# Two scratch tables in HBM stored with the heads as rows, and read back in 512-byte pieces

## The chip, the core and the metric

The kernel runs on one core of a Trainium2 chip. The metric is the device time of one execution in microseconds, in a median over runs. The core has a matrix engine (PE, with its weight loads listed as PEld), a vector engine (DVE), an activation engine (ACT), a general engine (POOL) and a queue engine (SP) that here only issues transfers. Sixteen DMA engines of the core carry out the transfers that SP and ACT issue.

## What is computed

The reference is one layer of a state-space mixer with a feed-forward part, on 2 sequences of 512 tokens with 512 channels. What bears on this case is the decay between tokens of a chunk:

```python
dt = clip(softplus(dt + dt_bias), 0, 100);  A_dt = dt * -exp(A_log)
A_cum = cumsum(A_dt, axis=-1)              # within a chunk of 128 tokens, per head
L = exp(_segsum(A_dt))                     # exp(A_cum[l] - A_cum[s]) for s <= l
Y_diag = einsum('bzlhn,bzshn,bhzls,bzshp->bzlhp', Cc, Bc, L, xch)
Y_off  = einsum('bzlhn,bzhpn,bhzl->bzlhp', Cc, prev, exp(A_cum))
```

There are 128 heads of 64 channels, 8 chunks of 128 tokens (4 of each sequence), and 8 groups that share B and C. Before this stands the input projection (512 to 18,560 columns), a causal convolution of 4 taps and a SiLU; behind it a gate, a group norm, the output projection (8192 to 512), a layer norm, a linear layer with low-rank additions and a second layer norm.

## The kernel before

A short first part, some 70 us long, projects the time steps (DT) and the first group's tiles, and computes the running sums A_cum for all heads at once: a tile of 128 heads x 1024 tokens (`sc[2]`) and its exponential (`sc[3]`). ACT writes both to scratch tables in HBM: `acum_d` (line 843) and `eacum_d` (line 857, in two transfers, even heads and odd heads). ACT also writes the small table `elast_d` (line 859).

Then come 8 groups of 16 steps. A step is a chunk c of a unit e (8 heads). Everything in the steps is laid out in the program; nothing is planned at run time, and each engine works through its own list, held by semaphores. In every step

- SP issues the loads in a fixed order (lines 448 to 470): `decay` for a later step, `eac` for the step after next where the chunk isn't a sequence's first, then the next weight tiles (`raw`, line 379), and now and then output weights (`wo_raw`, `c_new`, line 388) and a unit's small tables (`uch`, `tok`, `elast`).
- The load of `decay` (line 356) copies the A_cum of 8 heads of a chunk, 4 KB, to each of the 128 partitions. There are three slots: one for odd chunks, two for even ones. The load for an odd chunk is issued two steps ahead, for an even one four steps ahead, both once PE has read the slot's old content (`yd_ready`).
- The load of `eac` (line 365) copies exp(A_cum) of 4 heads, 2 KB, to each of 64 partitions, twice (even heads to the lower half, odd heads to the upper half).
- ACT subtracts (line 791, function `gaps`) and exponentiates (line 797) the decay, DVE multiplies it by C B^T (line 1125), and PE multiplies it with the inputs (line 654, `p_yd`). DVE scales the part from the state by `eac` (line 1151), and POOL adds it (line 1004).
- PE projects the weight tiles of the next unit: ACT rounds a loaded tile (`w_hi`, line 709), POOL takes the rest (`w_lo`, line 952), and PE does three matmuls of each (lines 495 to 497). A `raw` slot is loaded anew once both halves were taken from it.

`acum_d` lies by chunk first: (8 chunks, 128 heads, 128 tokens). `eacum_d` lies by chunk, then by even or odd head, then by head. So the 8 heads of a unit are contiguous within a chunk, and so are its 4 even ones.

Of the kernel before, what the change touches and what calls it, by code (L numbers as in the profile page):

```python
# [16 lines left out]
F32 = mybir.dt.float32  # L17
# [5 lines left out]
P = 128  # L23
BATCH, SEQ, HID = 2, 512, 512
TOK = BATCH * SEQ
KC = HID // P
HEADS, HD, NST, GROUPS, TAPS = 128, 64, 128, 8, 4
INTER = HEADS * HD
CHUNKS = TOK // P
CPB = CHUNKS // BATCH  # L30
UNITS = 2 * GROUPS
UH = HEADS // UNITS
UT = UH * HD // P
# [47 lines left out]
def wait(eng, sem, value):  # L81

    if not (isinstance(value, int) and value <= 0):
        eng.wait_ge(sem, value)
# [8 lines left out]
def mixer_ffn_kernel(nc, x_t, x_tok, w_t, unit_chan, group_chan, dt_bias, a_log, wo_t,  # L93
                     ffn_w, lora_a, lora_b, lora_w, ffn_bias, eye, upper, out):
    ctx = ExitStack()
    with ctx:
        def sb(name, shape, dt=F32):
            return ctx.enter_context(nc.sbuf_tensor(name, shape, dt))

        def sem(name):  # L100
            return ctx.enter_context(nc.semaphore(name))

        def pair(name):
            return [sem(f"{name}{i}") for i in range(2)]


        acum_d = nc.dram_tensor("acum_d", (CHUNKS, HEADS, P), F32, kind="Internal").ap()
        eacum_d = nc.dram_tensor("eacum_d", (CHUNKS, 2, HEADS // 2, P), F32, kind="Internal").ap()
        elast_d = nc.dram_tensor("elast_d", (HEADS, CHUNKS), F32, kind="Internal").ap()
        tok_d = nc.dram_tensor("tok_d", (P, UNITS, 3 * CHUNKS * UH), F32, kind="Internal").ap()  # L110

# [13 lines left out]
        decay = sb("decay", [P, 3, UH, P])  # L125
        eac = sb("eac", [P, 2, UT, P])
# [41 lines left out]
        raw_loaded, wo_loaded, decay_loaded, eac_loaded = pair("raw_loaded"), [sem(f"wo_loaded{i}") for i in range(UT)], [sem(f"decay_loaded{i}") for i in range(3)], pair("eac_loaded")  # L168
# [19 lines left out]
        acum_stored, eacum_stored, toks_stored = sem("acum_stored"), sem("eacum_stored"), sem("toks_stored")  # L188
# [11 lines left out]
        sc = [hs[:, 1, k, :] for k in range(UT)] + [half[:, 2 * k:2 * k + 2, :].rearrange("p a b -> p (a b)") for k in range(4)]  # L200
# [18 lines left out]
        def step(g, e, c):  # L219
            return g * 16 + (8 * e + c)  # L220

        def carried(g, e, c):

            return g * 12 + (6 * e + 3 * (c // CPB) + c % CPB)
# [18 lines left out]
        def dslot(c):  # L243

            return 0 if c % 2 else 1 + c // 2 % 2
# [105 lines left out]
        def load_decay(q, g, e, c):  # L351


            wait(q, yd_ready, step(g, e, c) - (1 if c % 2 else 3))
            src = acum_d[c, (2 * g + e) * UH:(2 * g + e + 1) * UH, :]
            q.dma_start(decay[:, dslot(c)].rearrange("p a b -> p (a b)"),
                        bass.AP(tensor=src.tensor, offset=src.offset, ap=[[0, P], [1, UH * P]])).then_inc(decay_loaded[dslot(c)], 16)

        def load_eac(q, g, e, c):

            slot = (carried(0, e, c) - 1) % 2
            wait(q, dh_ready, step(g, e, c) - 1)
            for h2 in range(2):
                src = eacum_d[c, h2, (2 * g + e) * UT:(2 * g + e + 1) * UT, :]
                q.dma_start(eac[h2 * HD:(h2 + 1) * HD, slot].rearrange("p a b -> p (a b)"),
                             bass.AP(tensor=src.tensor, offset=src.offset,
                                     ap=[[0, HD], [1, UT * P]])).then_inc(eac_loaded[slot], 16)


        @block.sync  # L370
        def _(sp):
# [37 lines left out]

            sp.wait_ge(acum_stored, 16)  # L410
            load_decay(sp, 0, 0, 0)
            load_w(None, PROLOGUE[9])
            load_decay(sp, 0, 0, 2)
            load_w(None, PROLOGUE[10])
            load_decay(sp, 0, 0, 1)
            sp.wait_ge(eacum_stored, 48)
            for slot in range(2):
                sp.wait_ge(unit_loaded[slot], 16)
                load_elast(sp, slot, slot)
            load_eac(sp, 0, 0, 1)  # L420
            load_w(0, LOOP_TILES[0])
            sp.wait_ge(tok_laid, 4)
# [24 lines left out]
            def body(g, last):  # L447
                for e in range(2):
                    for c in range(8):
                        od, ed, cd = ahead(e, c, 2 if c % 2 else 4)  # L450
                        if not (last and od):
                            load_decay(sp, g + od, ed, cd)
                        o2, e2, c2 = ahead(e, c, 2)
                        if c2 % CPB and not (last and o2):
                            load_eac(sp, g + o2, e2, c2)
                        for t in tiles_of(e, c, last):
                            off, n = divmod(t.n + 4, GRP_TILES)
                            if not (last and off):
                                load_tile(g + off, LOOP_TILES[n], last)
                        if c == 7 and not last:  # L460
                            load_channels(sp, 2 * g + (e + 2), e)
                            load_unit(sp, 2 * g + (e + 2), e)
                        if e == 0 and c == 4 and not last:
                            load_group(sp, g + 1)
                        if last and (e, c) == (1, 1):

                            sp.wait_ge(gated, step(GROUPS - 1, 1, 0))
                            for dst, src in ((ffn_w_sb, ffn_w), (lora_a_sb, lora_a), (lora_b_sb, lora_b),
                                             (bias_sb, bass.AP(tensor=ffn_bias.tensor, offset=0, ap=[[0, P], [1, HID]])),
                                             (lw[:], lora_w)):  # L470
                                sp.dma_start(dst, src).then_inc(ffn_loaded, 16)
# [231 lines left out]
        def _(act):  # L703
# [7 lines left out]
            def drain_proj(g, t, items=(0, 1)):  # L711

                for i, b in enumerate(t.batches):
                    if i not in items:
                        continue
                    act.wait_ge(proj_ready, item_n(g, t, i) + 1)
                    src = proj[bank(t, i)][:]
                    u, us = unit_of(g, t), uslot_of(t)
                    cols = slice(b * SEQ, (b + 1) * SEQ)
                    if t.kind in ("G0", "G1"):  # L720

                        wait(act, gated, 8 * u if t.kind == "G1" else 8 * u - 4)
                        nc.scalar.activation(gate[:, b, t.j, :], src, ACT.Silu).then_inc(proj_free[bank(t, i)], 1)
                        continue
                    if t.kind == "H":
                        wait(act, gated, 8 * u - 8)
                        dst, w, bias = hs[:, us, t.j, cols], conv_w(us, t.j, 3), conv_w(us, t.j, 4)
                        act.wait_ge(unit_loaded[us], chan_count(g, t))
                    else:
                        k = "BC".index(t.kind)  # L730
                        if t.kind == "C":
                            wait(act, c_ready, 0 if g is None else 2 * g + 2)
                            wait(act, wo_lo_ready, 0 if g is None else (2 * g + 2) * UT)
                        dst, w, bias = (bT, c_new)[k][:, cols], gch[:, k, 3:4], gch[:, k, 4:5]
                        act.wait_ge(group_loaded, 16 if g is None else 16 * g + 32)
                    nc.scalar.activation(dst, src, ACT.Identity, scale=w, bias=bias).then_inc(tap3_done, 1)  # L736
# [103 lines left out]
            drain_proj(None, PROLOGUE[4])  # L840
            silus(None, [PROLOGUE[3]])
            act.wait_ge(scanned, 2)
            act.dma_start(acum_d.rearrange("c h l -> h c l"), sc[2].rearrange("h (c l) -> h c l", c=CHUNKS)).then_inc(acum_stored, 16)
            drain_proj(None, PROLOGUE[5], (0,))
            v = sc[4].rearrange("p (c l) -> p c l", c=CHUNKS)
            a = sc[2].rearrange("p (c l) -> p c l", c=CHUNKS)
# [6 lines left out]
            nc.scalar.activation(sc[3], sc[2], ACT.Exp).then_inc(act_pre, 1)  # L853
            lay_tokens(1, 0)
            act.wait_ge(act_pre, 7)
            for h2 in range(2):
                act.dma_start(eacum_d[:, h2].rearrange("c a l -> a c l"),
                              sc[3][h2:HEADS:2].rearrange("a (c l) -> a c l", c=CHUNKS)).then_inc(eacum_stored, 16)
            act.dma_start(elast_d, elc[:]).then_inc(eacum_stored, 16)
            drain_proj(None, PROLOGUE[6], (0,))  # L860
            lay_tokens(2, 2)
# [540 lines left out]
```

## Time and profile before

| | |
|---|---|
| median of 3 runs | 1650.03 us (1648.02 to 1651.37) |
| the profiled execution | 1651.37 us, its span 1648.4 us |
| PE busy | 1614.3 us, 98% of the span |
| PEld, DVE, ACT, POOL busy | 78%, 82%, 74%, 62% |
| granted clock of PE, mean | 0.996 |
| DMA | 178.65 MB in 87144 packets, 108 GB/s over the span |

Each engine's row in the profile gives the time in which it had an instruction under way. Matmuls overlap one another, so that a busy PE is one with work in it, and not one at its peak. A DMA packet is here one piece of a transfer that is contiguous on both sides. The time "to landing" of a transfer runs from its issue to the last of its bytes, with the work that lay ahead of it in the DMA engines.

### The profile page before, as it was taken

How to read it: one execution, taken by the hardware profiler on the slowest of the kernel's cores; microseconds unless marked ns; L12 is line 12 of the kernel's file. 1: busy time of each engine (PE TensorE's matmuls, PEld its weight loads, DVE VectorE, ACT ScalarE, POOL GpSimd, SP SyncE). 2: the span in 40 equal slices, each digit the busy share in tenths (PEclk: the TensorE clock that was granted, in tenths of full speed). 3: DMA queues.
4: the chain of work that ended last, by engine and by line, in shares of the span. 5: the costliest groups of instructions: out<-in, count | busy, mean ns of one | idle time of the engine just before them, and what ended most of it. 6: DMA issues, size and time to landing. Idle time of an engine off the chain costs nothing. (4 is left out here: it accounts for less than half of the span.)

```text
span 1648.4 us, 26983 instructions
## 1 busy us (share of the span) xinstructions
PE 1614.3 (98%) x9072; PEld 1292.7 (78%) x9072; DVE 1348.8 (82%) x1855; ACT 1221.5 (74%) x2373; POOL 1021.2 (62%) x829
## 2 busy tenths in 40 slices
PE   7999999999999999999999999999999999999898
PEld 6777888778888788878887788887887878877655
DVE  5677798869987799877988689986998879887876
ACT  5868778776777877776787777788677778777742
POOL 4456667566675757656665656756566666666654
PEclk9999999999999999999999999999999999999999
DMA  3633324333242333423243333433323332333301
GB/s 125 238 110 103 113 84 157 88 103 103 84 158 84 113 96 107 132 91 113 92 123 118 99 100 94 145 97 113 99 100 120 103 119 94 108 110 102 128 27 45
DMA packets 87144, 178.65 MB, mean 108 GB/s; under 512 B 16480, under 2 KB 20576, under 8 KB 86624
## 3 DMA queue, kind: packets, MB, share of 16 engines
q1 hardware_dynamic: 83760, 175.72, 33.7%
q8 instruction: 73, 1.20, 0.3%
q10 hardware_dynamic: 3248, 1.22, 0.3%
q14 instruction: 63, 0.52, 0.1%
HBM read 172.17 MB, written 4.72 MB: 107 GB/s over the span
## 5 line engine op out<-in xcount | busy, mean ns | idle before, releaser
L952 POOL TENSOR_TENSOR w_lo<-raw,w_hi 128x512 fp32r<-128x512 f32 x209 | 297.9, 1426 | 295.5 <-ACT w_hi L709 294.5
L495 PE MATMUL proj<-x_hi,w_hi 128*128 128x512 f32 x1160 | 462.8, 399 | 8.5 <-DVE x_lo L1216 6.9
L496 PE MATMUL proj<-x_lo,w_hi 128*128 128x512 f32 x1160 | 452.9, 390 | 0.0
L497 PE MATMUL proj<-x_hi,w_lo 128*128 128x512 f32 x1160 | 452.8, 390 | 0.0
L1103 DVE SCALAR_TENSOR_TENSOR hs<-proj,uch,hs 128x511 f32<-128x511 f32 (+2 forms) x384 | 285.4, 744 | 56.9 <-ACT hs L736 51.6
L791 ACT ACTIVATE decay<-decay,tok 128x128 f32<-128x128 f32 x1024 | 312.5, 392 | 0.0
L1004 POOL TENSOR_TENSOR dh<-dh,eac 128x512 f32<-128x512 f32 x96 | 127.8, 1331 | 228.5 <-DVE eac L1151 228.4
L495 PEld LDWEIGHTS proj<-x_hi,w_hi 128*128 128x128 f32 x1160 | 218.9, 189 | 50.8 <-issue 6.9
L1125 DVE TENSOR_TENSOR decay<-decay,cb 128x1024 f32<-128x1024 f32 x128 | 190.9, 1491 | 80.2 <-ACT decay L797 77.7
L497 PEld LDWEIGHTS proj<-x_hi,w_lo 128*128 128x128 f32 x1160 | 218.3, 188 | 46.0
L496 PEld LDWEIGHTS proj<-x_lo,w_hi 128*128 128x128 f32 x1160 | 219.0, 189 | 41.6
L542 PE MATMUL p_out<-wo_hi,g_hi 128*128 128x512 f32 x512 | 211.7, 413 | 4.8 <-issue 4.8
L544 PE MATMUL p_out<-wo_hi,g_lo 128*128 128x512 f32 x512 | 201.8, 394 | 0.0
L543 PE MATMUL p_out<-wo_lo,g_hi 128*128 128x512 f32 x512 | 200.7, 392 | 0.0
L736 ACT ACTIVATE hs<-proj,uch 128x512 f32<-128x512 f32 x128 | 99.3, 776 | 133.0 <-PE proj L497 131.7
L1047 POOL TENSOR_TENSOR y<-y,gate 128x512 f32<-128x512 f32 x128 | 169.3, 1323 | 17.7 <-DVE y L1266 17.6
L709 ACT ACTIVATE w_hi<-raw 128x512 fp32r<-128x512 f32 x196 | 122.3, 624 | 68.8 <-PE proj L497 68.5
L969 POOL TENSOR_TENSOR xd<-xdt,tok 128x512 f32<-128x512 f32 x96 | 147.9, 1540 | 1.6 <-DVE xdt L1114 1.6
L975 POOL TENSOR_TENSOR dh<-hs,uch 128x512 f32<-128x512 f32 x128 | 148.4, 1159 | 0.7 <-ACT hs L746 0.7
L654 PE MATMUL p_yd<-decay,xdt 128*64 128x128 f32 x2048 | 140.1, 279 | 0.0
L1266 DVE TENSOR_TENSOR y<-p_yd,dh 128x512 f32<-128x512 f32 x128 | 87.8, 686 | 61.2 <-PE p_yd L654 56.5
L1306 DVE TENSOR_TENSOR g_lo<-y,g_hi 128x512 fp32r<-128x512 f32 x128 | 111.5, 871 | 27.0 <-ACT g_hi L911 27.0
(121 smaller groups left out, 2765.7 us busy)
## 6 DMA issues: line engine op xcount, KB each, us to landing
decay<-acum_d SPq DMA_DIRECT2D x128, 512.0 KB, 4.0
raw<-w_t SPq DMA_DIRECT2D x209, 256.0 KB, 2.8
eac<-eacum_d SPq DMA_DIRECT2D x192, 128.0 KB, 4.1
wo_raw<-wo_t SPq DMA_DIRECT2D x32, 256.0 KB, 3.6
c_new<-wo_t SPq DMA_DIRECT2D x32, 256.0 KB, 4.8
hs<-x_t SPq DMA_DIRECT2D x8, 256.0 KB, 5.3
acc<-x_tok SPq DMA_DIRECT2D x1, 2048.0 KB, 8.6
out<-acc SPq DMA_DIRECT2D x8, 256.0 KB, 2.0
```

Source lines behind the costliest of these rows:

```text
L495: nc.tensor.matmul(dst[:], w_hi[:, ws, k, :], x_hi[:, k, cols], start=(k == 0), stop=False)
L496: nc.tensor.matmul(dst[:], w_hi[:, ws, k, :], x_lo[:, k, cols], start=False, stop=False)
L497: mm = nc.tensor.matmul(dst[:], w_lo[:, ws, k, :], x_hi[:, k, cols], start=False, stop=(k == KC - 1))
L542: nc.tensor.matmul(p_out[:], g_hi[:, sl, j, :], wo_hi[:, j, :], start=(j == 0), stop=False)
L543: nc.tensor.matmul(p_out[:], g_hi[:, sl, j, :], wo_lo[:, j, :], start=False, stop=False)
L544: mm = nc.tensor.matmul(p_out[:], g_lo[:, sl, j, :], wo_hi[:, j, :], start=False, stop=(j == UT - 1))
L791: ins = nc.scalar.activation(decay[:, dslot(c), h, :], decay[:, dslot(c), h, :], ACT.Relu, scale=-1.0, bias=tok[:, e, 0, c, h:h + 1])
L952: nc.gpsimd.tensor_tensor(w_lo[:, s].rearrange("p a b -> p (a b)"), raw[:, s, :], w_hi[:, s].rearrange("p a b -> p (a b)").bitcast(F32), A ...
L975: nc.gpsimd.tensor_tensor(dh[:], hs[:, e, :, c * P:(c + 1) * P], bcast(d_skip(e), 2, P), ALU.mult).then_inc(dskip_done if c % CPB else dh_ ...
L1047: nc.gpsimd.tensor_tensor(y[:], y[:], gate[:, c // CPB, :, (c % CPB) * P:(c % CPB + 1) * P], ALU.mult).then_inc(gated, 1)
L1103: nc.vector.scalar_tensor_tensor(out=dst[:, shift:], in0=src[:, :SEQ - shift], scalar=w, in1=dst[:, shift:], op0=ALU.mult, op1=ALU.add).th ...
L1125: nc.vector.tensor_tensor(decay[:, dslot(c)], decay[:, dslot(c)], bcast(cb[:, c, :], 1, UH), ALU.mult).then_inc(mix_ready, 1)
```

## The change

Both tables are now (128 heads, 1024 tokens), which is how the tiles stand on the chip. The stores are one transfer each, of 128 rows of 4 KB. The loads pick the chunk out of each head's row: 8 pieces of 512 bytes for each partition in `decay`, and 4 pieces of 512 bytes for each partition in `eac`. The bytes moved are the same. There is one store less, and SP waits for a count of 32 and not 48 before it reads `elast_d`.

```diff
-        acum_d = nc.dram_tensor("acum_d", (CHUNKS, HEADS, P), F32, kind="Internal").ap()
-        eacum_d = nc.dram_tensor("eacum_d", (CHUNKS, 2, HEADS // 2, P), F32, kind="Internal").ap()
+        acum_d = nc.dram_tensor("acum_d", (HEADS, TOK), F32, kind="Internal").ap()
+        eacum_d = nc.dram_tensor("eacum_d", (HEADS, TOK), F32, kind="Internal").ap()
...
-            src = acum_d[c, (2 * g + e) * UH:(2 * g + e + 1) * UH, :]
-            q.dma_start(decay[:, dslot(c)].rearrange("p a b -> p (a b)"),
-                        bass.AP(tensor=src.tensor, offset=src.offset, ap=[[0, P], [1, UH * P]])).then_inc(decay_loaded[dslot(c)], 16)
+            src = acum_d[bass.ds((2 * g + e) * UH, UH), c * P:(c + 1) * P]
+            q.dma_start(decay[:, dslot(c)], bass.AP(tensor=src.tensor, offset=src.offset,
+                                                     ap=[[0, P], [TOK, UH], [1, P]])).then_inc(decay_loaded[dslot(c)], 16)
...
-                src = eacum_d[c, h2, (2 * g + e) * UT:(2 * g + e + 1) * UT, :]
-                q.dma_start(eac[h2 * HD:(h2 + 1) * HD, slot].rearrange("p a b -> p (a b)"),
+                src = eacum_d[bass.ds((2 * g + e) * UH + h2, 1), c * P:(c + 1) * P]
+                q.dma_start(eac[h2 * HD:(h2 + 1) * HD, slot],
                              bass.AP(tensor=src.tensor, offset=src.offset,
-                                     ap=[[0, HD], [1, UT * P]])).then_inc(eac_loaded[slot], 16)
+                                     ap=[[0, HD], [2 * TOK, UT], [1, P]])).then_inc(eac_loaded[slot], 16)
...
-            sp.wait_ge(eacum_stored, 48)
+            sp.wait_ge(eacum_stored, 32)
...
-            act.dma_start(acum_d.rearrange("c h l -> h c l"), sc[2].rearrange("h (c l) -> h c l", c=CHUNKS)).then_inc(acum_stored, 16)
+            act.dma_start(acum_d, sc[2]).then_inc(acum_stored, 16)
...
-            for h2 in range(2):
-                act.dma_start(eacum_d[:, h2].rearrange("c a l -> a c l"),
-                              sc[3][h2:HEADS:2].rearrange("a (c l) -> a c l", c=CHUNKS)).then_inc(eacum_stored, 16)
+            act.dma_start(eacum_d, sc[3]).then_inc(eacum_stored, 16)
```

No instruction changes its place. On SP, in the second half of the first group, a step's loads stood in this order before (the sizes are partitions x elements):

```order
L356 DMA decay<-acum_d 128x1024
L365 DMA eac<-eacum_d 64x512 x2
L379 DMA raw<-w_t 128x512 x2
L388 DMA wo_raw<-wo_t 128x512 x2
L379 DMA raw<-w_t 128x512
```

And so they stand now:

```order
L356 DMA decay<-acum_d 128x8x128
L365 DMA eac<-eacum_d 64x4x128 x2
L379 DMA raw<-w_t 128x512 x2
L388 DMA wo_raw<-wo_t 128x512 x2
L379 DMA raw<-w_t 128x512
```

The order is the same, and a weight tile still stands right behind the tables' loads. A partition's 1024 elements are now named as 8 runs of 128, and the 512 of `eac` as 4 runs of 128. On ACT, in the first part of the program, the two stores of `eacum_d` become one:

```order
 L804 ACTIVATE acc<-p_hid 128x4x16x8
 L804 ACTIVATE acc<-p_yd 128x4x16x8
-L857 DMA eacum_d<-hs 64x8x128 x2
-L859 DMA elast_d<-elc 128x8
+L856 DMA eacum_d<-hs 128x1024
+L857 DMA elast_d<-elc 128x8
 L736 ACTIVATE hs<-proj,uch 128x512
 L804 ACTIVATE acc<-p_hid 128x4x16x8
```

The store in 8 runs of 128 for each of 64 heads, twice, is now a store of 128 whole rows, and ACT has one issue less ahead of its next work on `proj`.

## Rows read from the trace of the kernel before

**Rows 1.** The profile page: busy time of the engines, and PE in 40 slices.

```profile
PE 1614.3 (98%) x9072; PEld 1292.7 (78%) x9072; DVE 1348.8 (82%) x1855; ACT 1221.5 (74%) x2373; POOL 1021.2 (62%) x829
PE   7999999999999999999999999999999999999898
```

**Rows 2.** Windows: length, busy us (x) of PE, PEld, DVE, ACT, POOL; PEclk, DMA share, GB/s.

```profile
60.00:70.00 10.00, 7.18 (x36) 5.77 (x35) 3.77 (x7) 8.59 (x15) 7.01 (x8) 1.00 0.88 301
...
200.00:600.00 400.00, 398.89 (x2282) 323.51 (x2281) 337.74 (x456) 309.41 (x600) 253.35 (x202) 1.00 0.34 107
```

**Rows 3.** DMA: the main queue; issues with KB each and median us to landing.

```profile
q1 hardware_dynamic: 83760, 175.72, 33.7%
...
decay<-acum_d SPq DMA_DIRECT2D x128, 512.0 KB, 4.0
raw<-w_t SPq DMA_DIRECT2D x209, 256.0 KB, 2.8
eac<-eacum_d SPq DMA_DIRECT2D x192, 128.0 KB, 4.1
...
tok<-tok_d SPq DMA_DIRECT2D x14, 96.0 KB, 2.4
...
acum_d<-hs ACTq DMA_DIRECT2D x1, 512.0 KB, 4.1
```

**Rows 4.** Windows on three transfers: acum_d stored, the first decay loaded, eacum_d stored.

```profile
39.25:40.75 1.50, 1.50 (x8) 1.27 (x7) 0.74 (x1) 1.48 (x2) 0.00 (x0) 1.00 1.13 343
42.50:43.50 1.00, 1.00 (x7) 0.85 (x6) 0.00 (x0) 1.00 (x5) 0.92 (x2) 1.00 0.90 324
47.25:49.50 2.25, 2.25 (x16) 1.95 (x15) 0.95 (x2) 1.57 (x3) 1.05 (x2) 1.00 0.88 266
```

**Rows 5.** Lines 356 and 365: ns of an issue, min/median/max; first and last start.

```profile
L356 SPq DMA_DIRECT2D decay<-acum_d x128: 326/327/431, 41.4 to 1579.2; - x128
...
L365 SPq DMA_DIRECT2D eac<-eacum_d x192: 444/451/1006, 52.2 to 1584.3; - x192
```

**Rows 6.** Waits: an engine's for a DMA, and SP's: total, times, longest.

```profile
POOL w_hi L960 <- DMA raw<-w_t: 5.5, 2, 3.3
...
SPq L356 <- PE p_yd L654: 699.4, 110, 14.7
```

**Rows 7.** Near 843 us: issues on SP, landing of raw, work on ACT.

```profile
840.71 0.33 SPq L356 DMA_DIRECT2D decay<-acum_d  x1
841.49 1.09 SPq L365 DMA_DIRECT2D eac<-eacum_d  x2
...
843.07 0.33 SPq L379 DMA_DIRECT2D raw<-w_t  x1
...
DMA to landing us min/median/max: 5.3/5.3/5.3
...
850.32 0.62 ACT L709 ACTIVATE w_hi<-raw 128x512 fp32r<-128x512 f32 x1
850.84 0.97 ACT L791 ACTIVATE decay<-decay,tok 128x128 f32<-128x128 f32 x3
```

**Rows 8.** Near 1537 us: issue and landing of a decay, and its use on ACT.

```profile
1537.53 0.33 SPq L356 DMA_DIRECT2D decay<-acum_d  x1
...
DMA to landing us min/median/max: 3.8/3.8/3.8
...
1542.30 0.98 ACT L791 ACTIVATE decay<-decay,tok 128x128 f32<-128x128 f32 x3
```

**Rows 9.** First part: ACT around the eacum_d stores, and PE's wait.

```profile
46.21 0.64 ACTq L857 DMA_DIRECT2D eacum_d<-hs  x1
...
47.70 0.78 ACT L736 ACTIVATE hs<-proj,uch 128x512 f32<-128x512 f32 x1 [1.27 <-issue]
...
57.34 0.78 ACT L736 ACTIVATE hs<-proj,uch 128x512 f32<-128x512 f32 x1 [1.65 <-PE proj L497]
...
68.28 0.30 PE L507 MATMUL p_hid<-ident,hs 128*128 128x128 f32 x1 [2.82 <-ACT hs L746]
```

## The prediction

> **What bounds the kernel now.** I read the page first. PE is busy for 1614.3 us of a span of 1648.4, and its row of slices is 9 nearly everywhere but at the start and the end [rows 1]. The windows say the same more sharply: between 200 and 600 us PE idles for 400 - 398.89 = 1.1 us, while the DMA engines are busy for a third of the time (0.34, 107 GB/s) [rows 2]. So in the 16-step groups the kernel ends when PE ends, and a transfer costs time only if it lands so late that a step's input misses its engine. Then I read the waits for any that ended on a DMA: the largest is POOL's for the first weight tiles, 5.5 us in two waits at the very start [rows 6], ahead of both tables. No wait on `decay` or `eac` is there. SP is not short of time either: before the loads of `decay` it waits 699.4 us in total for PE to free a slot [rows 6]. What the change touches is thus off the path, and the question is how much of its cover the new form eats.
>
> **The price of a piece.** Each transfer runs on 16 DMA engines. A `decay` load was 128 pieces of 4 KB, 8 for each engine; it becomes 1024 pieces of 512 bytes, 64 for each engine. An `eac` load was 64 pieces of 2 KB, 4 for each engine; it becomes 16 pieces of 512 bytes for each engine. The trace has 512-byte pieces in the other direction, in the stores of the two tables. While `acum_d` is stored, the DMA engines move 343 GB/s at a share of 1.13 (records at the window's edges take it above 1), so 303 GB/s when busy; in the stores of `eacum_d` 266 at 0.88, so 302 [rows 4]. That is 19 bytes per ns for each engine, 27 ns a piece. The first `decay`, in 4 KB pieces, ran at 324 GB/s with a share of 0.90, so 360 GB/s, 22.5 bytes per ns: 182 ns for 4 KB, 91 ns for 2 KB [rows 4].
>
> - `decay`: 64 x 27 = 1.73 us in place of 8 x 182 = 1.46, so +0.27 us a load.
> - `eac`: 16 x 27 = 0.43 in place of 4 x 91 = 0.36, so +0.07 us a load, +0.14 for the pair.
> - In sum 128 x 0.27 + 192 x 0.07 = 48 us of DMA time, and the main queue's share goes from 33.7% [rows 3] to some 36.6%. Its packets go from 83760 [rows 3] to 83760 + 128 x 896 + 192 x 192 = 235312.
>
> That the store of 512 KB in 1024 pieces landed after 4.1 us and the load of 512 KB in 128 pieces after 4.0 [rows 3] fits such a small difference. No row shows a broadcast read in 512-byte pieces, so this price is the disputed one. Bounds from the rows: not below 22.8 ns (512 bytes at the rate of the 4 KB pieces, no cost at all), and at most 91 ns, if a piece cost what a 2 KB piece costs. A load of `tok`, whose pieces are 768 bytes for 128 partitions, lands after 2.4 us, and one of `raw`, with as many pieces of 2 KB, after 2.8 [rows 3], so small pieces are not as dear as large ones. I take 27 ns, the row with the same piece, and keep 91 ns for the range.
>
> The Trainium skill speaks against this change in one place. The measured table in "DMA: Bandwidth & Descriptors", section "Bandwidth", gives 138 GB/s for 64 KB over 128 partitions, which is 512 bytes each, and 341 GB/s for 1 MB. By that a piece of 512 bytes would take about 59 ns, and the place of rival 1 below would cost (96 x 59 ns - 2.18 - 1.95) x 8 = 12 us, 1662 (an estimate from that page). The store rows show 302 GB/s for many such pieces in a row, so this trace disagrees for stores; for loads no row decides.
>
> **What covers it: `raw`.** The loads wait in one line, so `decay` and the two `eac` delay the weight tile behind them by 0.27 + 0.14 = 0.41 us. The tightest place I found in the steps is near 843 us: `decay` is issued at 840.71, the `eac` pair from 841.49, `raw` at 843.07; it lands after 5.3 us, at 848.37, and ACT takes it at 850.32 [rows 7]. That leaves 1.95 us, and 1.54 after the change. If it were late, `w_hi`, then POOL's `w_lo` and PE's projection would be late. This place comes once in each of the 8 groups.
>
> **`decay` itself.** The load issued at 840.71 would land, with the median of 4.0 us [rows 3], at 844.7, and ACT reads it from 850.84 [rows 7]: 6.1 us of cover. The tightest is in the last group, where steps are short of projections: issued at 1537.53, landed after 3.8, used at 1542.30 [rows 8], so 0.97 us of cover against +0.27. Cost nothing. The `eac` loaded with it is used later in the same step than `decay`, and has more.
>
> **Issues on SP.** An issue of `decay` takes 0.33 us, of `eac` 0.45 [rows 5]; the issue of the strided store of `eacum_d` takes 0.64 [rows 9]. A source with one more level costs SP between nothing and 0.31 us for `decay` and 0.19 for each `eac`, so `raw` goes out at most 0.69 us later. With 0.41 that is 1.10 of 1.95 us. I take 0.1 us for each of the three, hidden by SP's waits.
>
> **The first part.** ACT has one issue of 0.64 us less, ahead of its work at 47.70, before which it stood 1.27 us over issues [rows 9]. That work can start 0.6 us or so earlier, at most 1.27. But ACT waits for PE's projection again at 57.34, for 1.65 us, and PE's next idle time, 2.82 us up to 68.28, is at the end of the ACT work that starts there [rows 9]. PE's pace up to 57.34 sets that, and PE is not helped. So the gain is 0, bounded by 1.27. The store of `acum_d` in 4 KB rows lands some 0.3 us earlier, which only adds cover to what is read from it. The stretch where DMA is fullest, 0.88 at 60 to 70 us [rows 2], holds no load of either table.
>
> **The sum.** 1651.37 (profiled execution, span 1648.4) + 0 + 0 + 0 = 1651.4. The profiled run is the slowest of the three, 1.3 us above their median of 1650.03, so the forecast of the median is 1650.0.
>
> **The rivals.**
>
> 1. *The pieces are dear, and `raw` comes late (slower).* It decides from the point where 96 pieces cost 2.18 + 1.95 us, that is 43 ns each. At 54 ns, twice the stores' price, the three loads take 5.18 us and not 2.18; `raw` is late by 3.00 - 1.95 = 1.05 us in each of 8 groups, and the one `decay` of the last group by 64 x 0.054 - 1.46 - 0.97 = 1.0: 8 x 1.05 + 1.0 = 9.4, so 1659. At 91 ns it would be (96 x 91 ns - 2.18 - 1.95) x 8 = 37 us from that place alone, some 1690 us. For it: a read has to fetch the same 512 bytes for all partitions from HBM, and no row shows that. Against it: the 27 ns of the stores, `tok` at 2.4 us.
> 2. *The gain in the first part gets through (slightly faster).* ACT's 1.27 us would reach PE at 68.28, and the time would be 1648.8. It would still count as no change. More could only come from faster reads of HBM, which a PE busy for 99.7% of a window can't use.
> 3. *SP's issues grow more than thought.* With 0.69 us and 0.41 the cover still holds, 1650; it would take 1.54 us more in a row of three issues to matter.
>
> **How the numbers follow.** A measurement of this kernel can't tell less than 0.2%, 3.3 us, from no change. The forecast, no change, has 0.84, rivals 2 and 3 within it; rival 1 beyond 3.3 us has 0.11; and 0.05 is for a gain beyond 3.3 us by something not seen here. The range takes the spread of the runs before (1648.0 to 1651.4), 1.3 us of gain below it, and above it a start of rival 1, at 49 ns 8 x 0.57 = 4.6 us: 1646.5 to 1654.5.
>
> **What would show it.** In the profile after: packets of the main queue near 235,000 and its share 36 to 39%; `decay` landing after some 4.3 us and `eac` after 4.4; the issues on SP below 0.65 us; no wait on a DMA in the steps; PE busy for over 398.5 us between 200 and 600 us. Wrong would be a median landing of `decay` above 6 us, waits of ACT's `w_hi` or POOL's work for `raw`, or a share above 45% with PE idle in the steps.

## The result: 1.1% slower

| | before | changed |
|---|---|---|
| median, us | 1650.38 (4 runs, 1648.02 to 1651.37) | 1667.89 (4 runs, 1665.75 to 1671.05) |
| ratio | | 1.0113, 95% interval 1.0098 to 1.0128 |
| span of the profiled execution, us | 1648.4 | 1668.4 |

The forecast was no change, 1650.0, with a range up to 1654.5. It was wrong. The profile page of the changed kernel first: busy time, the main queue, and the issues with their median time to landing.

```profile
PE 1615.9 (97%) x9072; PEld 1292.9 (77%) x9072; DVE 1346.1 (81%) x1855; ACT 1221.7 (73%) x2373; POOL 1025.9 (61%) x829
...
q1 hardware_dynamic: 235312, 175.72, 43.8%
...
decay<-acum_d SPq DMA_DIRECT2D x128, 512.0 KB, 8.8
raw<-w_t SPq DMA_DIRECT2D x209, 256.0 KB, 6.4
eac<-eacum_d SPq DMA_DIRECT2D x192, 128.0 KB, 8.6
```

PE is busy as long as before, within 1.6 us (1614.3 us before [rows 1]), so of the 20.0 us by which the span grew 18.4 are idle time of PE. The packets are the 235312 of the forecast. But `decay` lands after 8.8 us and not 4.0, and the weight tiles behind it after 6.4 and not 2.8 [rows 3]. The largest waits of the changed kernel that end on a DMA (total, times, longest), and the longest ones of PE between 200 and 1400 us:

```profile
ACT w_hi L709 <- DMA raw<-w_t: 41.0, 20, 3.8
POOL w_hi L958 <- DMA raw<-w_t: 11.7, 4, 3.5
...
PE p_misc L518 <- DVE var L1135: 7.9, 6, 1.5
PE p_out L542 <- issue: 5.9, 6, 1.0
```

Before, waits on a DMA came only at the start, the largest POOL's [rows 6]. PE's wait on `var` is new, and the one in front of `p_out` grew from 1.1 us in total to 5.9; each comes six times in 1200 us, once in a group. The windows from 200 to 1400 us, of before and then of the changed kernel, give the sum (length, then busy us of PE, PEld, DVE, ACT, POOL, clock, DMA share, GB/s):

```profile
200.00:1400.00 1200.00, 1196.61 (x6831) 969.58 (x6830) 1015.92 (x1371) 924.91 (x1798) 764.81 (x607) 1.00 0.34 108
```

```profile
200.00:1400.00 1200.00, 1182.83 (x6746) 957.18 (x6745) 997.82 (x1348) 912.31 (x1774) 759.81 (x599) 1.00 0.45 106
```

PE loses 13.8 us here, 2.3 in each of six groups. Of the other 4.6 us of new idle time, 1.9 fall between 1400 and 1500 us, 1.5 in the first 100 us and 1.3 behind 1500 us. The place within a group is the one that the forecast named as the tightest. Its rows in the changed kernel answer to [rows 7]: the issues on SP, the landing of that `raw`, then ACT, DVE and PE.

```profile
850.73 0.38 SPq L356 DMA_DIRECT2D decay<-acum_d  x1
851.51 1.24 SPq L365 DMA_DIRECT2D eac<-eacum_d  x2
853.10 0.33 SPq L379 DMA_DIRECT2D raw<-w_t  x1
...
DMA to landing us min/median/max: 10.6/10.6/10.6
...
863.71 0.63 ACT L709 ACTIVATE w_hi<-raw 128x512 fp32r<-128x512 f32 x1 [3.28 <-DMA raw<-w_t]
864.25 2.44 ACT L791 ACTIVATE decay<-decay,tok 128x128 f32<-128x128 f32 x8
...
869.09 1.47 DVE L1123 TENSOR_TENSOR decay<-decay,cb 128x1024 f32<-128x1024 f32 x1 [5.09 <-ACT decay L797]
...
873.56 1.10 PE L660 MATMUL p_st<-xd,b_tok 128*128 128x512 f32 x2 [0.57 <-DVE eac L1149]
876.58 0.46 PE L518 MATMUL p_misc<-cT,bT 128*128 128x128 f32 x2 [1.49 <-DVE var L1135]
880.89 0.47 PE L542 MATMUL p_out<-wo_hi,g_hi 128*128 128x512 f32 x1 [0.98 <-issue]
```

`raw` takes 10.6 us where it took 5.3, and had 1.95 us of cover: 3.3 us late, as ACT's wait says. ACT then does the decay of the next steps behind this wait, DVE waits 5.09 us for it, and 10 us later PE runs dry three times. The last of the three ends where DVE ends its late `wo_lo` (2.79 us from 878.00). In the six groups ACT's wait at this place is 2.2 to 3.3 us, 2.7 in the mean, and PE loses 2.3. ACT waits as long for `raw` at one more place of each group (3.82 us up to 782.14), but there it stood for PE before (3.14 us up to 771.00 in the kernel before), and PE shows no wait behind it.

### The profile page after: what moved, and what is told of

It is laid out like the page before. It is cut to its first block and busy times, and to the rows that moved or that the text cites. A ratio compares the mean times of both kernels' runs of the same rounds, so it can differ in the third digit from the quotient of the medians.

```text
span 1668.4 us, 26982 instructions
## 1 busy us (share of the span) xinstructions
PE 1615.9 (97%) x9072; PEld 1292.9 (77%) x9072; DVE 1346.1 (81%) x1855; ACT 1221.7 (73%) x2373; POOL 1025.9 (61%) x829
## 3 DMA queue, kind: packets, MB, share of 16 engines
q1 hardware_dynamic: 235312, 175.72, 43.8%
## 5 line engine op out<-in xcount | busy, mean ns | idle before, releaser
L950 POOL TENSOR_TENSOR w_lo<-raw,w_hi 128x512 fp32r<-128x512 f32 x209 | 292.6, 1400 | 312.9 <-ACT w_hi L709 311.9
L1123 DVE TENSOR_TENSOR decay<-decay,cb 128x1024 f32<-128x1024 f32 x128 | 186.6, 1458 | 103.2 <-ACT decay L797 100.7
L967 POOL TENSOR_TENSOR xd<-xdt,tok 128x512 f32<-128x512 f32 x96 | 154.8, 1612 | 1.2 <-DVE xdt L1112 1.2
L1304 DVE TENSOR_TENSOR g_lo<-y,g_hi 128x512 fp32r<-128x512 f32 x128 | 119.1, 930 | 27.0 <-ACT g_hi L909 27.0
```

The costliest lines, as they stand in the source:

```text
L950: nc.gpsimd.tensor_tensor(w_lo[:, s].rearrange("p a b -> p (a b)"), raw[:, s, :], w_hi[:, s].rearrange("p a b -> p (a b)").bitcast(F32), A ...
L967: nc.gpsimd.tensor_tensor(xd[:], xdt[:], bcast(tok[:, e, 2, c, :], 2, HD), ALU.mult).then_inc(xd_ready, 1)
L1123: nc.vector.tensor_tensor(decay[:, dslot(c)], decay[:, dslot(c)], bcast(cb[:, c, :], 1, UH), ALU.mult).then_inc(mix_ready, 1)
```

## The experiments

Each kernel was run beside the kernel before. The GB/s in the table are those of one window of 1 to 2.5 us inside the first load of `decay` at 42 to 46 us, where little else moves; the landing is the median of all 128 loads. In e4, e10 and e14 `decay` is loaded from other places of HBM, out of the weights `w_t`, and `eac` as in the changed kernel.

| kernel | rows shared by all partitions | pitch of the 8 pieces | GB/s | decay lands, us | median, us | ratio (95%) |
|---|---|---|---|---|---|---|
| changed | yes | 4096 | 86 | 8.8 | 1667.89 | 1.0113 (1.0098 to 1.0128) |
| e12 | yes | 4160 | 83 | 8.6 | 1665.59 | 1.0100 (1.0083 to 1.0116) |
| e11 | yes | 2048 | 174 | 6.2 | 1649.85 | 0.9997 (0.9987 to 1.0006) |
| e14 | yes | 128 K | 157 | 5.4 | 1651.15 | 1.0010 (1.0001 to 1.0019) |
| e3 | yes | 576 | 222 | 4.7 | 1648.41 | 1.0000 (0.9990 to 1.0009) |
| e13 | yes | 1024 | 312 | 4.0 | 1650.18 | 1.0004 (0.9995 to 1.0014) |
| e9 | yes | 4608 | 335 | 4.2 | 1649.29 | 0.9994 (0.9985 to 1.0003) |
| e15 | yes | 0 (one piece) | 43 | 16.0 | 2002.69 | 1.2133 (1.2100 to 1.2166) |
| e4 | no | 576 | 299 | 4.3 | 1649.38 | 1.0002 (0.9992 to 1.0011) |
| e10 | no | 4096 | 312 | 4.3 | 1650.08 | 0.9999 (0.9990 to 1.0008) |

A pitch is the distance from one piece's start to the next's, here between the 8 pieces of a partition. My first theory after the result, G, was that the pieces are handed out by one source at 170 a us, whatever they are.

**Which table.** The kernel before with one table in the new form.

```diff
# e1_decay_only: before, with the new acum_d, its store and load_decay
+        acum_d = nc.dram_tensor("acum_d", (HEADS, TOK), F32, kind="Internal").ap()
# e2_eac_only: the changed kernel, with acum_d, its store and load_decay as before
+        acum_d = nc.dram_tensor("acum_d", (CHUNKS, HEADS, P), F32, kind="Internal").ap()
```

> Only acum_d and the loads of decay take the new form (1024 pieces of 512 bytes a load); eacum_d and eac stay as before. Theory G (pieces are handed to the DMA engines one after another by one source that serves all 16 engines and both queues, at some 170 a us, so a decay takes 6 us whatever its addresses are): decay lands after 8 to 9 us, raw after a median of 5 to 6, the time is 1655 to 1663 us. Theory H (HBM serves many short reads of one place slowly, by address): the same here, since the addresses of decay are those of the changed kernel. Theory P (my price of 27 ns a piece on each engine, something else is slow): decay lands after 4.3, 1650 us.

> Only eacum_d and the loads of eac take the new form (256 pieces of 512 bytes a load, 64 before); decay stays in 128 pieces of 4 KB. Theory G: the pair of eac loads takes 512 / 170 = 3 us in place of 0.75, raw behind it lands after 5 to 6 us where it stands behind a pair, decay after 4 to 5; the cover of 1.95 us of raw is just used up, 1650 to 1655 us. Theory P: 1650 us, all landings within 0.3 us of before.

e1 ran in 1668.15 us (ratio 1.0116, 1.0100 to 1.0131), with `decay` landing after 8.9 us and `raw` after 6.5. e2 ran in 1649.39 (1.0000, 0.9991 to 1.0010), with `decay` after 3.7 and `eac` after 5.7. So the loads of `decay` make the whole loss; e1 is even above what G gave it. The new `eac` is slower too (5.7 against 4.1 us), but all of that is covered. In e2 `raw` lands after 3.0 us, where G had 5 to 6, so e2 speaks against G already; and the 5.7 us of `eac` lie outside what P allowed.

**Number of pieces, or addresses.** e3 keeps the pieces and changes the pitch; e4 lets each partition read its own rows.

```diff
# e3_near_pitch (both tables by chunk)
+        acum_d = nc.dram_tensor("acum_d", (CHUNKS, HEADS, P + 16), F32, kind="Internal").ap()
+                        ap=[[0, P], [P + 16, UH], [1, P]]
# e4_own_rows (source w_t)
+                        ap=[[(P + 16) * UH, P], [P + 16, UH], [1, P]]
```

> Both tables lie by chunk first again, as before, but each head's 512 bytes are followed by 64 unused bytes, so that the loads have as many pieces of 512 bytes as in the changed kernel, at a pitch of 576 bytes and not of 4 or 8 KB. Theory G (number of pieces): as the changed kernel, decay lands after 8 to 9 us, 1664 to 1671 us. Theory H (the pitch of 4 or 8 KB puts the pieces on the same part of HBM): decay lands after some 4.5 us, 1650 us.

> The loads of decay read, for each partition, its own stretch of the weights in 8 pieces of 512 bytes, in place of the same 8 rows of acum_d for all partitions (the decay values are thus not the right ones). As many pieces, no address read twice in a load. Theory G: as the changed kernel, 8 to 9 us to landing, 1664 to 1671 us. Theory H' (16 engines that read the same 512 bytes at once hold one another up): decay lands after some 4.5 us and the time is 1650 to 1655 us.

Both are as fast as before, so G fell: the pieces are as many (235312 packets in each), and the loss is gone. The windows of the first `decay` in the changed kernel, in e3 and in e4 show how the rate changed:

```profile
42.50:45.00 2.50, 2.50 (x13) 2.05 (x12) 0.95 (x2) 2.50 (x7) 1.08 (x1) 1.00 0.41 86
```

```profile
43.50:45.00 1.50, 1.50 (x8) 1.22 (x7) 0.09 (x1) 1.50 (x6) 0.98 (x1) 1.00 0.93 222
```

```profile
43.00:44.50 1.50, 1.50 (x8) 1.21 (x7) 0.30 (x1) 1.50 (x5) 0.76 (x1) 1.00 1.02 299
```

The DMA engines are busy for 0.41 of the time in the changed kernel: a piece keeps an engine busy for 39 ns (0.41 x 512 x 16 / 86), but comes only every 95 ns. For the rest of the time the engines have nothing under way that the trace shows, with a load in flight. e3 and e4 changed the pitch both, and e4 the sharing as well.

**Pitch, sharing, or both.** e9 pads the changed kernel's rows by 512 bytes, e10 keeps the pitch of 4096 with own rows, e11 has 2048.

```diff
# e9_row_pad_512 (acum_d and eacum_d)
+        acum_d = nc.dram_tensor("acum_d", (HEADS, TOK + 128), F32, kind="Internal").ap()
+            ap=[[0, P], [TOK + 128, UH], [1, P]]
# e10_own_rows_4k (source w_t)
+            ap=[[UH * TOK, P], [TOK, UH], [1, P]]
# e11_pitch_2k: as e3, with 4 * P for P + 16
```

> The changed kernel with each head's row in both tables followed by 512 unused bytes: a pitch of 4608 bytes (9216 for eac) in place of 4096 (8192). Same pieces, same order, same single stores. Theory A (a pitch of exactly 4 KB puts the 8 pieces of a partition on the same part of HBM): decay lands after 4.7 us, the waits for raw go, 1648 to 1651 us. Theory D (pieces spread over more than some KB are slow, whatever the pitch): as the changed kernel, 8 to 9 us, 1664 to 1671 us.

> The loads of decay read, for each partition, 8 rows of its own of the weights, 512 bytes each, at a pitch of 4096 bytes (the decay values are not the right ones). Theory A (the pitch alone is bad): as slow as the changed kernel or slower, decay lands after 8 us or more, 1664 us or more. Theory S (it takes both, the pitch and that all partitions read the same 8 rows): decay lands after 4.3 to 5 us as with own rows at 576 bytes, 1648 to 1652 us.

> Tables by chunk with a pitch of 2048 bytes between heads (512 used), 4096 between the heads that an eac load picks. Theory A with a part of HBM for each so many KB: 2 KB spreads the 8 pieces of decay over two such parts where 4 KB had one, so decay lands after 5.5 to 7 us, and the time is 1650 to 1658 us. If only 4 KB and its multiples matter, decay lands after 4.7 us and the time is 1648 to 1651 us.

e9 takes the whole loss away (1649.29 us; PE is busy for 1196.54 us from 200 to 1400 us, as before), and D fell. e10 does so at the old pitch (1650.08), and A fell as I had put it: the pitch alone does no harm. It takes shared rows at that pitch, theory S. e11 lies between: 6.2 us to landing, and no time lost, since the cover holds. The windows of e9, e10 and e11:

```profile
42.50:43.50 1.00, 1.00 (x7) 0.83 (x6) 0.00 (x0) 1.00 (x4) 0.92 (x2) 1.00 1.10 335
```

```profile
43.00:44.00 1.00, 1.00 (x6) 0.83 (x5) 0.13 (x1) 1.00 (x4) 0.42 (x1) 1.00 1.04 312
```

```profile
42.50:44.00 1.50, 1.50 (x8) 1.25 (x7) 0.34 (x1) 1.50 (x5) 0.71 (x1) 1.00 0.61 174
```

Half the pitch gives twice the rate, 174 for 86.

**How the rate follows from the addresses.** Four more pitches, the last of them zero.

```diff
# e12_row_pad_64: as e9, with TOK + 16
# e13_pitch_1k: as e3, with 2 * P for P + 16
# e14_far_shared_rows (source w_t)
+            ap=[[0, P], [32 * TOK, UH], [1, P]]
# e15_one_piece (source acum_d)
+            ap=[[0, P], [0, UH], [1, P]]
```

> As the kernel with 512 unused bytes behind each row, but with 64: a pitch of 4160 bytes. The 8 pieces of a decay load are shifted by 448 bytes in all. Theory C (the part of HBM follows from the address in steps of some 512 bytes within 4 KB, and one part serves some 170 reads a us): the pieces reach over two steps at best, decay lands after 6 to 8.5 us, 1652 to 1668 us. If any pitch other than a power of two does: 4.3 us, 1650.

> Tables by chunk with a pitch of 1024 bytes between heads (512 used). Theory C: with 4 parts and not 2 (pitch 2048) or 1 (4096) the pieces start at up to 680 a us, more than the 16 engines take at 27 ns each (590), so decay lands after 4.3 to 4.8 us, eac (pitch 2048) after 5 to 6, 1648 to 1651 us. If a power of two as such is bad: 6 us as with 2048.

> All partitions read the same 8 pieces of 512 bytes, at a pitch of 128 KB (rows of the weights, so the decay values are not the right ones). Theory C with higher address bits that choose the part too: fast, decay lands after 4.3 us, 1650 us. If what hurts is that all engines ask for the same piece at the same time, or that only the place within 4 KB counts: as the changed kernel, some 170 pieces a us, 8.8 us, 1664 to 1671.

> The loads of decay read one piece of 512 bytes (the unit's first head) for all 8 heads and all 128 partitions, at the changed kernel's place (the decay values are not the right ones). If one part of HBM serves some 170 reads a us whatever they ask for: as the changed kernel, decay lands after 8.8 us, 1664 to 1671 us. If changing between 8 far rows of HBM is what costs: faster than 6 us, 1650 to 1655 us.

The windows of e15, e12, e14 and e13:

```profile
44.00:46.00 2.00, 2.00 (x10) 1.65 (x9) 0.43 (x1) 2.00 (x6) 1.14 (x1) 1.00 0.21 43
```

```profile
42.50:45.00 2.50, 2.50 (x12) 2.06 (x11) 1.04 (x2) 2.50 (x7) 0.99 (x1) 1.00 0.67 83
```

```profile
42.50:43.50 1.00, 1.00 (x6) 0.82 (x5) 0.00 (x0) 1.00 (x4) 0.87 (x1) 1.00 0.56 157
```

```profile
43.50:45.00 1.50, 1.50 (x9) 1.24 (x8) 0.00 (x0) 1.50 (x5) 1.33 (x2) 1.00 1.03 312
```

One piece that all 128 partitions read 8 times comes at 43 GB/s, half the rate of the changed kernel, so far rows of HBM are not what costs; they help. e15 missed both of its readings, the whole kernel too: `decay` lands after 16.0 us, and the time is 2002.69 us. The rates 43, 86, 174 read like 1, 2 and 4 places that each give 43 GB/s, until the 16 engines bound it (over 300, at a share of about 1). A shift of 64 bytes a row does not help (83), one of 512 does (335). e14 at 157 came between its two readings: the place within 4 KB is not all that counts, but it is half as fast as the engines could be.

The places are a reading of the rates, and not shown. What a place is, in the memory or on the way to it, no run here shows; nor does any run show whether a place is slow for all reads or only for repeated reads of the same bytes, since the own rows of e4 and e10 are not read twice in a load. And the reading does not give every rate: e3 has 222 GB/s at a share of 0.93, so that a piece keeps an engine busy for 34 ns (0.93 x 512 x 16 / 222), and in e12 it is 66 ns (0.67 x 512 x 16 / 83), against 27 in e9. Both have shared rows whose starts are no multiples of 512 bytes; with own rows at the pitch of e3, in e4, it is 28 ns. The cause of these longer pieces is open.

**Where the loss gets to PE.** e5 is the changed kernel with `raw` issued ahead of the pair of `eac`.

```diff
# e5_raw_before_eac, in SP's step
-                        if c2 % CPB and not (last and o2):
-                            load_eac(sp, g + o2, e2, c2)
                         for t in tiles_of(e, c, last):
...
+                        if c2 % CPB and not (last and o2):
+                            load_eac(sp, g + o2, e2, c2)
```

> The changed kernel with the weight tiles' loads (raw) ahead of the pair of eac loads in every step on SP, still behind decay. If the time is lost because raw lands late behind the tables' loads, raw gains the 1 to 2 us of the eac loads, the waits of w_hi for raw fall from 41 us to under 15, and the time to 1653 to 1660 us; eac has over 5 us of cover to give. If the loss is elsewhere (decay itself late, or the engines slowed), the time stays at 1664 to 1671.

It ran in 1655.22 us (1.0028, 1.0018 to 1.0037): 12.7 of the 17.5 us come back by an order of issue, with `decay` landing as late as in the changed kernel (8.8 us). ACT's waits for `raw` fell only to 23.7 us, where I had expected under 15, but PE is busy for 1193.55 us from 200 to 1400 us, where the changed kernel had 1182.83. PE's longest waits of e5 between 200 and 1400 us:

```profile
PE p_out L542 <- issue: 3.9, 6, 1.0
PE p_hid L507 <- ACT hs L746: 2.4, 6, 0.4
```

The wait on `var` is gone (7.9 us in the changed kernel), and ACT's wait at the forecast's place fell, near 853 us, to 0.52 us. No kernel here beats the one before: e9, which has the single stores of the change and its pitch mended, is at 0.9994 (0.9985 to 1.0003), no difference.

## Why the prediction was wrong

- **What bounds the kernel** was right: PE, idle for 3.4 us of 1200 before, and a transfer costs nothing until it lands too late.
- **The price of a piece** is the step that failed. I took 27 ns from stores. For the DMA engines alone that was right: in e9 the main queue's share is 36.7% and `decay` lands after 4.2 us, against a forecast of 36.6% and 4.3. But what a load gets also depends on where the bytes that it reads lie. In the changed kernel the pieces came at 86 GB/s, 95 ns for each engine's piece (512 x 16 / 86). That is above the 91 ns that I had set as the upper bound, because I took that bound from the first `decay` of the kernel before, whose 4 KB lie in one stretch. I also said that I kept 91 ns for the range, but the range ended at 49 ns, 1654.5; 91 ns would have been 1690. Rival 1, dear pieces and a late `raw`, is the case that came true, and I gave it 0.11. Its reason, that all partitions read the same bytes, is half of the cause: shared rows at 1024 or 4608 bytes are fast (e13, e9), own rows at 4096 too (e10), and it takes both, the sharing and the pitch.
- **The cover of `raw`**: the place and the 1.95 us were right, to 0.1 us (3.28 late of 5.3 longer). The way was not. I had it go through `w_lo` to PE's projection; it went through ACT's own line, where the decay of the next steps stands behind `w_hi`. Rival 1's sum would be too much: at 91 ns it gave 37 us, with `raw` 4.6 us late in each group, and it was 2.7 in the mean, of which PE lost 2.3. One part of the difference is `eac`: with the old `eac`, in e1, ACT waits 2.72 us there and not 3.28, so the new one adds 0.6 us, where 91 ns would have made it 2.2.
- **`decay` in the last group**: 0.97 us of cover was used up once, a wait of ACT of 4.2 us in the changed kernel, as rival 1 had it in kind (1.0 us at 54 ns a piece, 3.7 at 95).
- **SP's issues** grew to 0.38 and about 0.62 us, within the bounds, and cost nothing (e9).
- **The first part**: no gain. PE is busy for 33.06 us between 60 and 100 us of the changed kernel, for 34.28 in the kernel before.
- **The Trainium skill's table** in "DMA: Bandwidth & Descriptors", section "Bandwidth", measured on transfers that the general engine issued, would have given 59 ns and 1662 us (an estimate from that page). e9 shows 335 GB/s for 512-byte pieces of a 512 KB load, so its 138 GB/s for 64 KB is not a rate of the pieces. It would have pointed in the right direction by the wrong cause. The same page, section "Latency and other measured facts", tells of row pitches at large powers of two that slow copies, more so from 2 MiB up, healed by a pad of 4 KiB and not by 192 bytes. No run here has pitches that large. What is alike is that the pitch decides: shared rows at 4 KB are slow, a pad of 64 bytes leaves them so (83 GB/s), and one of 512 bytes heals them (335).

## What to carry to other kernels

When many partitions read the same few rows of HBM, look at where those rows lie, not only at how many pieces there are: try a pad behind each row (512 bytes on rows of 4096 here), or keep what is read together contiguous. A piece's price in the DMA engine is a lower bound; a share of 0.41 with a load in flight says that something other than this price sets the rate. And work out the cover of what stands behind the changed transfer, then try the order of issue: it gave back 12.7 of 17.5 us.

## What the runs showed of the hardware

- 16 DMA engines that all read one piece of 512 bytes get 43 GB/s in all; 8 shared pieces at 4096 bytes' pitch 86, at 2048 174, at 128 K 157, at 1024 312 and at 4608 335.
- A 512-byte piece of a load keeps an engine as busy as one of a store: 27 ns in e9 (512 x 16 x 1.10 / 335). With shared rows it was more in the changed kernel (39), in e3 (34) and in e12 (66).
- A slow load of `decay` goes with a late transfer on the other queue too; by what path, no run here shows. The store of `eacum_d`, on ACT's queue, in 4 KB pieces, was the same in the changed kernel, in e2 and in e15, and in e9 but for the 512 unused bytes behind each row. It landed after 3.7 us in e2, whose `decay` is as before, after 4.1 in e9, after 23.6 in e15, and in the changed kernel after 9.1:

```profile
eacum_d<-hs ACTq DMA_DIRECT2D x1, 512.0 KB, 9.1
```
